# Row maxima of an attention layer folded piece by piece on GpSimd and turned on VectorE, instead of reduced on VectorE and turned on TensorE

## The chip, the cores and the metric

The kernel runs on one core of one Trainium2 chip. TensorE (PE), VectorE (DVE), ScalarE (ACT), GpSimd (POOL) and SyncE (SP, which issues nearly all DMAs here) run side by side and meet at semaphores. The metric is the device time in microseconds (us), median of several executions.

## The reference

One transformer layer in float32: attention, a layer norm, a linear layer with quantised operands, a second layer norm. Only the attention scores bear on the change:

```
# B=2 batches, H=16 heads, DK=16, L=2048, D=256
scores = einsum('bhqd,bhkd->bhqk', Q, K) / sqrt(DK)
scores = scores * tau[..., None] + delta[:, :, None, :]
attn   = softmax(scores, axis=-1)
out    = einsum('bhqk,bhkd->bhqd', attn, V)
x = layernorm(x + out @ out_w.T + out_b)
x = layernorm(x + ffn(x))
```

The softmax subtracts each query row's maximum over 2048 keys before the exponential. The kernel computes the scores twice: once with queries on the partitions, only to find the row maxima, and once with keys on the partitions, with the negated maximum already added by the matmul, for the exponential.

## The kernel before

A first block (about 250 us) makes Q, K, V, tau and delta and stores Q and K, split in high and low parts, in DRAM. The second block is the attention, with the rest of the layer at its end. Heads go in groups of 4 (`HG`), the 2048 queries of a group in 4 quarters of 512, so there are `NIT` = 32 iterations i. `q_set` and `k_set` hold two groups at a time (two heads on partitions 0 to 63, two on 64 to 127). Rows 0 to 47 of each half are the operand, two more rows of `k_set` carry delta, and rows `ROW_MAX`, `ROW_MAX`+1 of `q_set` carry the negated row maximum, high and low part.

The work of an iteration is written as 32 slots (`SLOTS`, two to each key tile k). TensorE does in a slot, in this order:

- a PV half (line 937): 8 matmuls of exponentials and values, into bank 0;
- an ST pair (line 924): two score tiles, keys on partitions, two key tiles (`AHEAD`) before they are used. So the first ST of iteration i+1 stands in slot 28 of iteration i. It waits for `rows_set`, the DMAs that bring the maxima into `q_set`. ScalarE takes each tile through the exponential (line 1069); three banks are shared, so an ST waits for the exponential three tiles back;
- what is due of a list `items` (lines 179 to 189), a hand-written order for TensorE and VectorE alike.

`items` holds for each quarter j 32 units. A unit is two score tiles with queries on the partitions (`s_unit`, line 227) into one of two bank pairs, and one VectorE reduction of both to a maximum each (`max_unit`, line 237, into `mx`). A unit may go to TensorE once VectorE has freed the pair of two items back (`s_free`). Four units (4 key chunks of 512) make the maxima of 128 queries of two heads. Units run ahead: when iteration i starts, units up to (i+1, `LEAD`) are issued, with `LEAD` 12.

Once unit (j, 31) is reduced, the maxima go to `q_set` in five steps: VectorE reduces `mx` over the 4 chunks to `nm` (`row_maxima`, line 260); GpSimd splits it in high and low (`split_max`, lines 85 and 89) into `nm_pad`; TensorE transposes `nm_pad` into a bank pair as a 33rd item "rows", after unit (j+1, 2) (`rows_turn`, line 244); VectorE copies 32 rows of it to `nm_rows` (`rows_copy`, line 252); SP issues four DMAs (`rows_store`, line 278). The last "rows" item, of j = 31, has no units beside it and is preceded by 8 score matmuls that nobody reads (`unread`, line 883).

The slot of an item follows from `due`: items in this iteration, spread evenly over the slots. With 33 items for 32 slots, slot 31 gets two. ScalarE's evacuation of bank 0 at the end of an iteration (`evacuate`, line 1058) stands in its order behind the exponentials of slot 30's ST; the first PV half of the next iteration waits for it (`att_evac`).

Other users of the queues: SP loads the next head group at the start of every fourth iteration (`group_load`, 14 DMAs, lines 165 and 168) and stores the evacuated tile (lines 1377, 1379); GpSimd copies the values of the next group in every fourth iteration (`refill`, line 1326) and normalises late chunks (line 1350). VectorE has pieces of the linear layer mixed in from iteration 27 on.

## Time and profile before

| | |
|---|---|
| runs, us | 1684.31, 1676.60, 1676.23; median 1676.6 |
| the profiled execution, us | 1681.14 |
| its span, first to last instruction, us | 1679.1 |
| mean granted TensorE clock | 0.982 |
| busy, us (share of the span) | PE 1634.2 (97%), DVE 1526.7 (91%), ACT 1311.7 (78%), POOL 127.8 (8%) |
| chain that ended last, by engine | PE 60%, DVE 23% |

Busy time of TensorE is the time in which any matmul record is open, and ends of matmuls are modelled, so a share of 97% does not say how fast it works. What follows goes by the starts of the matmuls. "Idle before" is the idle time of an engine just ahead of an instruction, with what ended it behind the arrow.

### The profile page before, as it was taken

How to read it: one execution, taken by the hardware profiler on the slowest of the kernel's cores; microseconds unless marked ns; L12 is line 12 of the kernel's file. 1: busy time of each engine (PE TensorE's matmuls, PEld its weight loads, DVE VectorE, ACT ScalarE, POOL GpSimd, SP SyncE). 2: the span in 40 equal slices, each digit the busy share in tenths (PEclk: the TensorE clock that was granted, in tenths of full speed). 3: DMA queues.
4: the chain of work that ended last, by engine and by line, in shares of the span. 5: the costliest groups of instructions: out<-in, count | busy, mean ns of one | idle time of the engine just before them, and what ended most of it. 6: DMA issues, size and time to landing. Idle time of an engine off the chain costs nothing.

```text
span 1679.1 us, 33556 instructions
## 1 busy us (share of the span) xinstructions
PE 1634.2 (97%) x13879; PEld 733.6 (44%) x13884; DVE 1526.7 (91%) x1648; ACT 1311.7 (78%) x2375; POOL 127.8 (8%) x166
## 2 busy tenths in 40 slices
PE   8999989999999999999999999999999999999987
PEld 7777753333333333333333333333333343333466
DVE  5789876999999999999999999999999989898887
ACT  3876736888888888888888888888888876678645
POOL 4222213000000000000000000000010000000110
PEclk9999996999999999999999999999999999999989
DMA  3365426000600060024003300422051001010312
GB/s 112 106 179 156 141 81 108 8 8 8 85 9 8 18 75 8 15 27 66 9 8 43 53 8 8 57 39 60 31 70 23 8 8 46 8 39 13 120 59 88
DMA packets 46960, 84.72 MB, mean 50 GB/s; under 512 B 9116, under 2 KB 21020, under 8 KB 44092
## 3 DMA queue, kind: packets, MB, share of 16 engines
q1 hardware_dynamic: 44952, 82.49, 22.9%
q8 instruction: 109, 1.79, 0.5%
q14 instruction: 43, 0.35, 0.1%
q10 hardware_dynamic: 1856, 0.09, 0.1%
HBM read 51.36 MB, written 30.67 MB: 49 GB/s over the span
## 4 chain that ended last, share of the span: by engine, by line
PE 60%; DVE 23%; issue 1%; ACT 0%; ACTq 0%; POOL 0%; DVEq 0%
PE ps L937 25%; DVE mx L237 20%; PE ps L924 20%; PE ps L227 11%; PE ps L870 2%; PE ps L868 1%; PE ps L990 1%; PE ps L244 0%; PE ps L984 0%; PE ps L867 0%; DVE stats L1173 0%; DVE work L1221 0%; DVE work L1232 0%; DVE small L1216 0%; ACT e L1038 0%
## 5 line engine op out<-in xcount | busy, mean ns | idle before, releaser
L237 DVE TENSOR_REDUCE mx<-ps 128x2 f32<-128x1024 f32 x1024 | 1226.3, 1222 | 74.8 <-PE ps L227 66.6
L1069 ACT ACTIVATE e<-ps 128x512 f32<-128x512 f32 x2048 | 1109.7, 596 | 235.4 <-PE ps L924 197.6
L937 PE MATMUL ps<-e,v_grp 128*32 128x256 f32 x8192 | 662.6, 394 | 0.3 <-issue 0.2
L924 PE MATMUL ps<-q,k 52*128 52x512 f32 x2048 | 527.2, 502 | 4.5 <-PEq L355 4.3
L227 PE MATMUL ps<-k,q 50*128 50x512 f32 x2048 | 420.2, 405 | 11.3 <-DVE mx L237 8.6
L924 PEld LDWEIGHTS ps<-q,k 52*128 52x128 f32 x2048 | 200.4, 184 | 434.1 <-ACT e L1069 390.3
L937 PEld LDWEIGHTS ps<-e,v_grp 128*32 128x32 f32 x8192 | 162.7, 108 | 358.9 <-issue 210.9
L227 PEld LDWEIGHTS ps<-k,q 50*128 50x128 f32 x2048 | 197.5, 188 | 42.6 <-DVE mx L237 32.7
L684 PE MATMUL ps<-x_p,m_p 128*128 128x512 f32 x576 | 143.9, 404 | 0.0
L684 PEld LDWEIGHTS ps<-x_p,m_p 128*128 128x128 f32 x576 | 108.2, 192 | 33.3 <-issue 9.0
L525 DVE SCALAR_TENSOR_TENSOR hid<-x_c,dw_w,hid 128x512 f32<-128x512 f32 x128 | 103.8, 861 | 15.6 <-ACT hid L466 15.5
L472 ACT ACTIVATE hid<-hid 128x512 f32<-128x512 f32 x64 | 40.5, 632 | 51.4 <-DVE hid L525 50.1
L85 POOL CAST nm_pad<-nm 128x16 fp32r<-128x16 f32 x32 | 6.7, 210 | 885.2 <-DVE nm L260 885.2
L466 ACT ACTIVATE hid<-x_c,dw_b,dw_w 128x512 f32<-128x512 f32 x64 | 46.6, 804 | 0.2
L1326 POOL COPY v_grp<-v_all 128x272 f32<-128x272 f32 x32 | 13.7, 433 | 316.8 <-PE ps L937 316.7
L870 PE MATMUL ps<-wo_t,v_all 128*128 128x256 f32 x128 | 34.0, 389 | 0.0
L707 PE MATMUL ps<-hid,pw_w 128*16 128x512 f32 x128 | 29.7, 594 | 0.0
L1350 POOL TENSOR_TENSOR v_all<-v_all 128x1024 f32<-128x1024 f32 x8 | 19.7, 2465 | 119.6 <-DMA v_all<-rz_rows 119.6
L870 PEld LDWEIGHTS ps<-wo_t,v_all 128*128 128x128 f32 x128 | 25.2, 197 | 3.7
L698 PEld LDWEIGHTS ps<-wv_p,x_p 128*128 128x128 f32 x192 | 26.1, 197 | 1.4
L698 PE MATMUL ps<-wv_p,x_p 128*128 128x256 f32 x192 | 26.7, 290 | 0.0
L990 PE MATMUL ps<-fw_p,xq_t 128*128 128x256 f32 x128 | 19.6, 310 | 7.0 <-ACT xq_t L1051 7.0
(142 smaller groups left out, 610.3 us busy)
## 6 DMA issues: line engine op xcount, KB each, us to landing
k<-k_parts SPq DMA_DIRECT2D x42, 256.0 KB
q<-q_parts SPq DMA_DIRECT2D x42, 256.0 KB
k_parts<-k_sp SPq DMA_DIRECT2D x16, 512.0 KB, 5.0
q_parts<-q_sp SPq DMA_DIRECT2D x16, 512.0 KB, 4.1
att<-ev SPq DMA_DIRECT2D x32, 256.0 KB
x_c<-in_x_t SPq DMA_DIRECT2D x8, 514.0 KB, 5.7
tau_r<-tau_rows SPq DMA_DIRECT2D x16, 256.0 KB
x_in<-in_x SPq DMA_DIRECT2D x8, 512.0 KB, 3.9
```

The lines of the kernel that those rows point to most:

```text
L227: last = nc.tensor.matmul(ps[:, s_bank(s) + half, :], q_set[r, g % 2, jh, lo + qt * P:lo + (qt + 1) * P], k_set[r, g % 2, jh, kc * CH:(kc ...
L237: nc.vector.tensor_reduce(mx[:, j % 2, :, jh, qt, kc], ps[:, b0:b0 + 2, :], AX.X, ALU.max).then_inc(s_free, 1)
L466: nc.scalar.activation(hid[:, k, c, r], x_c[:, n % 2, c, 1:1 + CH], ACT.Identity, bias=dw_b[:, k, c, r:r + 1], scale=dw_w[:, k, c, r, 1:2] ...
L472: nc.scalar.activation(hid[:, k, c, r], hid[:, k, c, r], ACT.Gelu).then_inc(gelu_done, 1)
L525: nc.vector.scalar_tensor_tensor(y_, x_c[:, n % 2, c, which:which + CH], dw_w[:, k, c, r, which:which + 1], y_, ALU.mult, ALU.add).then_in ...
L684: mm = nc.tensor.matmul(ps[:, o, :], m_p[:, kw, side, c, tap, P * o:P * (o + 1)], x_p[:, n % 2, kx_, c, tap:tap + CH], start=(m == 0), sto ...
L698: last = nc.tensor.matmul(ps[:, v_bank(n, v), D * a:D * (a + 1)], x_p[:, n % 2, kx_, c, lo:lo + P], wv_p[:, kw, c, :], start=(m == 0), sto ...
L870: last = nc.tensor.matmul(dst, a_t[p][:, c, P * a:P * (a + 1)], wo_t[:, c, :], start=False, stop=(c == CT - 1))
L924: nc.tensor.matmul(ps[:, st_bank(n), :], k_set[r, g % 2, jh, kt * P:(kt + 1) * P], q_set[r, g % 2, jh, lo:lo + CH], start=True, stop=True) ...
L937: last = nc.tensor.matmul(ps[32 * h:32 * (h + 1), 0, PVW * part:PVW * (part + 1)], v_grp[:, kt, h, :], e[:, x % E_BUFS, h * CH + PVW * par ...
L990: last = nc.tensor.matmul(tok(f_bank(n), a), xq_t[:, n % 2, a, c, :], fw_p[:, part, c, :], start=False, stop=(c == CT - 1 and part == 1), ...
L1069: nc.scalar.activation(e[:, x % E_BUFS, h * CH:(h + 1) * CH], ps[:, st_bank(n), :], ACT.Exp).then_inc(e_ready, 1)
```

## The change

- `row_maxima`, `rows_copy`, the "rows" items and `unread` are gone. An iteration has 32 items instead of 33, all units (some late iterations have others besides).
- `fold` on GpSimd: for each of the 8 groups of four units two instructions take the larger of three chunks' maxima (one column on 128 partitions each), and after a wait two more take in the fourth and negate. That is 32 instructions per quarter j, 1024 in all. Groups 3 to 7 of j = i+1 and 0 to 2 of j = i+2 are folded in iteration i, two per quarter iteration, ahead of that quarter's refill. `split_max` follows group 7.
- `rows_turn` is now a VectorE transpose of 32x32 blocks of a 128x32 tile, `nm_pad` to `nm_rows`, behind unit (j+1, 1). At the end it stands behind `gathered(0, 1)` and `gathered(0, 2)` and ahead of `z_reciprocal(dve, 1)`.
- `rows_store` is eight DMAs of 16 runs of 128 B, where it was four of 8 runs of 512 B. `q_set` is laid out by quarter and then head, so that its runs merge; a group load then has 20 DMAs instead of 14 (q by head, in runs of 2 KB where they were 8 KB).
- `LEAD` 14 (was 12), `DEFER` 2 (was 3); the units of iteration 30 are spread over 5/8 of its slots (was 3/4).

```diff
-GROUP_DMAS = 2 * (2 * TERMS + 1)
+GROUP_DMAS = 2 * (TERMS + HH * TERMS + 1)
...
-        q_set = sb(top, "q_set", [P, 2, HH, L], F32R)
+        q_set = sb(top, "q_set", [P, 2, NQ, HH, CH], F32R)
...
+                    for jh in range(HH):
+                        eng.dma_start(q_set[rows, g % 2, chunks, jh, :].bitcast(F32),
+                                      q_parts[Q_PARTS[r], b, heads.start + jh, :, cols].rearrange("d (c l) -> d c l", l=CH)).then_inc(done, 16)
...
-        LEAD = 12
-        DEFER = 3
+        LEAD = 14
+        DEFER = 2
...
-                if u == DEFER - 1 and j > 0:
-                    items.append((j - 1, "rows"))
...
+        FOLD_AHEAD = LEAD // 4
+        FOLD_ORDER = [(qt, jh) for qt in range(TT) for jh in range(HH)]
...
-        ROWS_INC = 16 * HG
+        ROWS_INC = 16 * 2 * (P // BLOCK)
...
+        def fold(pool, j, n):
+
+            qt, jh = FOLD_ORDER[n]
+            done = 2 * (len(FOLD_ORDER) * j + n + 1)
+            pool.wait_ge(s_free, unit_at[j, qt, jh, NQ - 1] + 1)
+            rows = [((half * HH + jh) * TT + qt, mx[:, j % 2, half, jh, qt]) for half in range(2)]
+            for r, parts in rows:
+                nc.gpsimd.tensor_scalar(mn[:, r:r + 1], parts[:, 0:1], parts[:, 1:2], parts[:, 2:3], ALU.max, ALU.max).then_inc(mx_folded, 1)
+            pool.wait_ge(mx_folded, done)
+            for r, parts in rows:
+                nc.gpsimd.tensor_scalar(nm[:, r:r + 1], mn[:, r:r + 1], parts[:, 3:4], -1.0, ALU.max, ALU.mult).then_inc(nm_max, 1)
...
+        def rows_turn(dve, j):
+
+            dve.wait_ge(nm_ready, j + 1)
+            if j > 0:
+                dve.wait_ge(rows_set, j * ROWS_INC)
+            nc.vector.transpose(nm_rows[:].bitcast(F32), nm_pad[:].bitcast(F32)).then_inc(nm_turned, 1)
...
+            for half in range(2):
+                row = HALF * half + ROW_MAX
+                rows = q_set[row:row + 2, g % 2, j % NQ].rearrange("t j (q l) -> t (j q) l", q=TT)
+                for b in range(P // BLOCK):
+                    first = BLOCK * b + BLOCK // 2 * half
+                    sp.dma_start(rows[:, :, BLOCK * b:BLOCK * (b + 1)].bitcast(F32), nm_rows[first:first + BLOCK // 2, :].bitcast(F32)).then_inc(rows_set, 16)
...
-                        goal = items.index((i + 2, LEAD)) if i + 2 < NIT else len(items) - 1
+                        goal = items.index((i + 2, LEAD)) if i + 2 < NIT else len(items)
                         due = goal - issued
-                        slots = SLOTS * 3 // 4 if i == NIT - 2 else SLOTS
+                        slots = SLOTS * 5 // 8 if i == NIT - 2 else SLOTS
...
-                            if u == UNITS - 1:
-                                row_maxima(dve, s)
+                            if u == DEFER - 1:
+                                rows_turn(dve, j - 1)
...
+                            for group in (FOLD_AHEAD + 2 * c, FOLD_AHEAD + 2 * c + 1):
+                                j = i + 1 + group // len(FOLD_ORDER)
+                                if j < NIT:
+                                    fold(pool, j, group % len(FOLD_ORDER))
+                                if group == len(FOLD_ORDER) - 1 and j < NIT:
+                                    split_max(pool, j)
```

**TensorE, slot 31 of iteration 1.** Before; L937 is the PV half (4 heads), L924 the ST pair, L227 the score tiles of a unit, two to each. The rows are slots 30, 31 and the PV half of the next iteration:

```order
270 L937 MATMUL ps<-e,v_grp 32x256 x4
271 L924 MATMUL ps<-q,k 128x512 x2
272 L227 MATMUL ps<-k,q 128x512 x2
273 L937 MATMUL ps<-e,v_grp 32x256 x4
274 L924 MATMUL ps<-q,k 128x512 x2
275 L227 MATMUL ps<-k,q 128x512 x4
276 L937 MATMUL ps<-e,v_grp 32x256 x4
```

Now the same slots, where L918 is the PV half and L905 the ST pair:

```order
268 L918 MATMUL ps<-e,v_grp 32x256 x4
269 L905 MATMUL ps<-q,k 128x512 x2
270 L227 MATMUL ps<-k,q 128x512 x2
271 L918 MATMUL ps<-e,v_grp 32x256 x4
272 L905 MATMUL ps<-q,k 128x512 x2
273 L227 MATMUL ps<-k,q 128x512 x2
274 L918 MATMUL ps<-e,v_grp 32x256 x4
```

The second unit of slot 31 (x4 is two units) is gone; every slot of the iteration has one.

**VectorE, the first iterations of the attention.** Before; L237 is a unit's reduction:

```order
138 L1099 UNCONDITIONAL_BRANCH
139 L237 TENSOR_REDUCE mx<-ps 128x2 x23
140 L260 TENSOR_REDUCE nm<-mx 128x16
141 L237 TENSOR_REDUCE mx<-ps 128x2 x3
142 L252 CAST nm_rows<-ps 32x128
143 L237 TENSOR_REDUCE mx<-ps 128x2 x29
```

Now:

```order
136 L1078 UNCONDITIONAL_BRANCH
137 L237 TENSOR_REDUCE mx<-ps 128x2 x24
138 L268 STREAM_TRANSPOSE nm_rows<-nm_pad 128x32
139 L237 TENSOR_REDUCE mx<-ps 128x2 x32
140 L268 STREAM_TRANSPOSE nm_rows<-nm_pad 128x32
```

Two small instructions per quarter have become one, two units behind the quarter's last reduction instead of three.

**GpSimd, a later part of iteration 3.** Before, rows of iterations 1 to 3 stand together, since GpSimd has only the two splits and the refills (L1326):

```order
63 L85 CAST nm_pad<-nm 128x4x4
64 L89 TENSOR_TENSOR nm_pad<-nm,nm_pad 128x4x4
65 L1326 COPY v_grp<-v_all 128x16x17 x2
66 L85 CAST nm_pad<-nm 128x4x4
67 L89 TENSOR_TENSOR nm_pad<-nm,nm_pad 128x4x4
68 L1326 COPY v_grp<-v_all 128x16x17 x2
```

Now, from the second refill (L1303) of iteration 3 to behind its third; L248 and L251 are the two halves of a fold:

```order
143 L1303 COPY v_grp<-v_all 128x16x17
144 L248 TENSOR_SCALAR mn<-mx 128x1 x2
145 L251 TENSOR_SCALAR nm<-mn,mx 128x1 x2
146 L85 CAST nm_pad<-nm 128x2x8
147 L89 TENSOR_TENSOR nm_pad<-nm,nm_pad 128x2x8
148 L248 TENSOR_SCALAR mn<-mx 128x1 x2
149 L251 TENSOR_SCALAR nm<-mn,mx 128x1 x2
150 L1303 COPY v_grp<-v_all 128x16x17
151 L248 TENSOR_SCALAR mn<-mx 128x1 x2
```

The split now stands behind the last fold of its quarter (rows 144, 145) and ahead of the first of the next.

## Rows read from the trace of the kernel before

**Rows 1.** The page, busy us (share of the span) xinstructions.

```profile
PE 1634.2 (97%) x13879; PEld 733.6 (44%) x13884; DVE 1526.7 (91%) x1648; ACT 1311.7 (78%) x2375; POOL 127.8 (8%) x166
```

**Rows 2.** TensorE timeline, slots 23 to 0: start us, us, engine line op out<-in xcount.

```profile
701.53 0.33 PE L244 MATMUL ps<-ident_f,nm_pad 128*128 128x128 f32 x1
701.78 0.64 PE L937 MATMUL ps<-e,v_grp 128*32 128x256 f32 x8
...
707.31 0.50 PE L924 MATMUL ps<-q,k 52*128 52x512 f32 x2
...
710.46 0.64 PE L937 MATMUL ps<-e,v_grp 128*32 128x256 f32 x8
...
711.36 0.98 PE L227 MATMUL ps<-k,q 50*128 50x512 f32 x4
712.27 0.64 PE L937 MATMUL ps<-e,v_grp 128*32 128x256 f32 x8
```

**Rows 3.** Timeline of ScalarE there.

```profile
710.38 1.08 ACT L1069 ACTIVATE e<-ps 128x512 f32<-128x512 f32 x2 [0.21 <-PE ps L924]
711.35 0.60 ACT L1058 ACTIVATE ev<-ps 128x512 f32<-128x512 f32 x1
711.83 1.10 ACT L1069 ACTIVATE e<-ps 128x512 f32<-128x512 f32 x2
```

**Rows 4.** VectorE timeline, an iteration and a half; in brackets idle before, its releaser.

```profile
661.62 0.28 DVE L252 CAST nm_rows<-ps 32x128 fp32r<-32x128 f32 x1
...
698.17 0.22 DVE L260 TENSOR_REDUCE nm<-mx 128x16 f32<-128x64 f32 x1
...
701.89 0.28 DVE L252 CAST nm_rows<-ps 32x128 fp32r<-32x128 f32 x1
703.13 21.63 DVE L237 TENSOR_REDUCE mx<-ps 128x2 f32<-128x1024 f32 x18 [0.96 <-PE ps L227]
```

**Rows 5.** Line 252 between 298 and 1352 us: duration ns min/median/max, first and last start.

```profile
L252 DVE CAST nm_rows<-ps x27: 269/278/279, 298.3 to 1351.5; 32x128 fp32r<-32x128 f32 x27
```

**Rows 6.** The same view of line 237, 400 to 1300 us.

```profile
L237 DVE TENSOR_REDUCE mx<-ps x710: 1165/1226/1229, 399.9 to 1299.5; 128x2 f32<-128x1024 f32 x178
```

**Rows 7.** Timeline of GpSimd, a split.

```profile
738.97 0.20 POOL L85 CAST nm_pad<-nm 128x16 fp32r<-128x16 f32 x1 [6.69 <-DVE nm L260]
739.25 0.22 POOL L89 TENSOR_TENSOR nm_pad<-nm,nm_pad 128x16 fp32r<-128x16 f32 x1
```

**Rows 8.** Timeline of SP's DMA issues: a group load, stores of the maxima.

```profile
585.07 1.26 SPq L165 DMA_DIRECT2D k<-k_parts  x3
...
621.66 2.58 SPq L278 DMA_DIRECT2D q<-nm_rows  x4
...
702.20 2.56 SPq L278 DMA_DIRECT2D q<-nm_rows  x4
```

**Rows 9.** Issues of two lines: duration ns min/median/max, first and last start.

```profile
L278 SPq DMA_DIRECT2D q<-nm_rows x128: 596/612/716, 236.7 to 1549.9; - x128
L387 SPq DMA_DIRECT2D tau_r<-tau_rows x16: 577/592/726, 53.6 to 227.4; - x16
```

**Rows 10.** Stretches: length, busy us by engine, PEclk, DMA share, GB/s.

```profile
84.00:86.00 2.00, 2.00 (x17) 1.87 (x16) 2.00 (x2) 0.63 (x1) 1.92 (x2) 1.00 0.74 143
...
600.00:605.00 5.00, 5.00 (x56) 1.83 (x48) 4.95 (x5) 4.39 (x9) 0.00 (x0) 1.00 0.99 116
...
610.00:615.00 5.00, 5.00 (x45) 1.80 (x42) 4.45 (x4) 3.88 (x9) 0.00 (x0) 1.00 0.55 102
```

**Rows 11.** The same view of a stretch with a store of the maxima.

```profile
661.90:665.00 3.10, 3.10 (x36) 1.21 (x28) 2.13 (x2) 2.70 (x6) 0.00 (x0) 1.00 0.03 9
```

**Rows 12.** Timeline of TensorE in iterations 30 and 31.

```profile
1545.89 1.09 PE L883 MATMUL ps<-k,q 50*128 50x512 f32 x8
...
1547.51 0.64 PE L937 MATMUL ps<-e,v_grp 128*32 128x256 f32 x8
...
1567.29 0.27 PE L867 MATMUL ps<-bias,ones 128*128 128x256 bf16 x1 [1.47 <-issue]
```

118 lines of the change are left out of this document (37 added, 81 removed).

## Prediction, made before the changed kernel ran

> **What bounds the kernel now.** First the page's busy shares [rows 1]: TensorE 97%, VectorE 91%, ScalarE 78%. Two engines are candidates, so the timelines decide. On TensorE a slot (PV half, ST pair, one unit) takes 1.24 us: from slot 24 at 701.78 to slot 31 at 710.46 there are seven, 8.68 us [rows 2], and none has a gap. VectorE, when it has something to catch up, does a reduction every 1.20 us (18 in 21.63) [rows 4]. So in a plain slot TensorE sets the pace, and VectorE has 0.04 us to spare. The granted clock is 1.00 (2.4 GHz) in all stretches shown after 600 us [rows 10, 11].
>
> An iteration without a disturbance lasts 40.27 us, from one `rows_copy` to the next (661.62 to 701.89) [rows 4]. 32 slots of 1.24 are 39.68. Of the 0.59 left, slot 31 takes 0.57: it has two units and lasts 1.81 (710.46 to 712.27) [rows 2]. The transpose stands in the place of a unit and costs about what a unit costs. The mean of 26 iterations is (1351.5 - 298.3) / 26 = 40.51 [rows 5], so 0.24 more goes to scattered waits that the change does not name.
>
> **What the change takes away.** VectorE loses 0.22 + 0.28 us of small work per iteration and the 0.96 us in which it waited because the transpose slot brought it no unit [rows 4]; it gets one transpose of 128x32, which the trace does not show. Its nearest rows are the 0.22 reduction and the 0.28 copy; I take 0.2, with 0.15 and 0.3 as ends. But VectorE does not set the pace: 32 x 1.20 + 0.2 = 38.6 against TensorE's 39.68. This saving is hidden, and the 0.3 us are worth nothing where TensorE is first.
>
> TensorE loses the 33rd item, so slot 31 has one unit. That alone would give 0.57 + 0.02 us. What is late next? **ScalarE's evacuation of bank 0.** It stands behind the exponentials of slot 30, starts at 711.35 and ends at 711.95 [rows 3]. The first PV half of the next iteration waits for it. With one unit in slot 31 that PV half would be ready at 710.46 + 1.24 = 711.70. It finds bank 0 still unread, and starts at 711.95 plus a hand-over; GpSimd's from its own instruction to the next is 739.25 - 739.17 = 0.08 [rows 7], I take 0.07. So 0.32 us of the 0.59 come back as a wait, and 0.27 stay. Today the second unit covers the evacuation entirely. ScalarE's place is fixed by slot 30's ST, which keeps its distance, so the wait does not shrink by itself.
>
> This holds for iterations 1 to 23 and 25, 24 of them: 24 x 0.27 = **6.5 us**. Iteration 24 has the item "ft" besides and keeps a double slot; in 26 the same number of other items falls due.
>
> **The rest of the sum.** Iterations 27 to 29 have VectorE full of the linear layer's work. There its small work counts: 0.5 - 0.2 = 0.3 at least, 1.3 if the 0.96 us wait goes too; I take 0.5, nearer the lower end, since other waits stand there: **1.5 us**. In iteration 30 the 8 unread matmuls start at 1545.89 and the next PV half at 1547.51 [rows 12], held up by the reduction, the split and the transpose; without them it could follow the ST at once: **1.5 us**. The chain that ends in the wait of 1.47 us at 1567.29 [rows 12] starts with that store of the maxima. It moves forward, since the last unit is issued four slots sooner (5/8 against 3/4), and SP's four further issues (2.6 us) take back half of that; so PE does not merely meet the same data later. In iteration 0 all 36 items are units (35 before), and VectorE is behind there: 1.23 + 0.2 - 0.22 - 0.28 - 0.41 of waiting is **0.5 us lost**. Sum: 6.5 + 1.5 + 1.5 - 0.5 = 9.0 us.
>
> **What is hidden, and under what.** *The way of the maxima* must end before the first ST of the next iteration, in slot 28 at 707.31 [rows 2]. Today the copy starts at 701.89, 0.11 behind the start of slot 24, SP issues from 702.20 to 704.76, and the ST is not held up [rows 2, 4, 8]. So landing takes at most 2.55 us. Now the last unit ahead of the turn is issued in slot 19 instead of 22: the turn starts 0.11 behind slot 21. That leaves 7 x 1.24 + 0.57 - 0.11 = 9.14 us. It needs 0.2 (turn) + 0.03 + 8 x 0.64 (2.56 / 4 [rows 8]) + 2.55 = 7.90. Spare: 1.24 us. The price of an issue rests on this: 8 runs cost 0.61, and `tau_r`, with 128 partitions, 0.59 [rows 9]. The number of runs doesn't set it. So 0.64 stands, and per-run pricing (1.28) is the upper end.
>
> The engines' share during a store is 0.03 over 3.1 us [rows 11]: 0.03 x 3.1 x 16 / 32 runs = 0.047 us a run of 512 B. The Trainium skill, page "DMA: Bandwidth & Descriptors", section Specifications, says that runs under 512 B are not at line rate, as the DMA engine reads, modifies and writes. No row here shows 128 B runs. By that rule I estimate 0.09 us a run; if two engines did all 128 of them, that is 6.0 us against 5.1 of issues, and the spare falls from 1.24 to 0.3. The sum stays, the rival below gets a larger chance.
>
> *GpSimd's chain.* The last reduction of a quarter ends 2.5 us ahead of the turn (two slots). The last fold and the split need 0.07 + 2t + 0.08 + 2t + 0.08 + 0.20 + 0.08 + 0.22 = 0.73 + 4t. Every small GpSimd instruction takes 0.20 to 0.22 [rows 7]; with t = 0.2 it is 1.5 us. VectorE waits from t = 0.44 on. Behind its turn are queued the reductions that free TensorE's bank pairs, with 0.8 us to spare (needed 0.91 into a slot, done at 0.08), so TensorE feels it from t = 0.65. The other seven folds lie over four slots each and cost nothing. Contention: GpSimd's copies and splits lie beside the 710 reductions between 400 and 1300 us, and none exceeds 1229 ns against a median of 1226 [rows 6].
>
> The Trainium skill, page "GPSIMD Engine Reference", section 7, gives about 102 cycles for each small read command, which does not overlap the one before. A fold has two more operands by address; at the page's 1.2 GHz I estimate t = 0.37 and a chain of 2.2 us, still under 2.5. By either the sum is the same, by the page with 0.3 us to spare.
>
> *Group loads* are 20 issues instead of 14 on SP, 6 x 0.42 (1.26 / 3 [rows 8]) = 2.5 us; behind them is queued the store of the evacuated tile, needed 40 us later. The load starts at 585.07, keeps the engines at 0.99 and ends near 612.8 [rows 8, 10]; the maxima follow at 621.66, in future some 3.5 us sooner. 5 us are spare, 19% of the load. Runs of 2 KB moved 143 GB/s at a share of 0.74, runs of 8 KB 116 at 0.99 [rows 10], so shorter runs are no dearer. In the first block SP issues 2.5 us more in four chunks, ahead of stores that are wanted a chunk later: nothing.
>
> **Rivals.**
> 1. *The evacuation does not hold TensorE up* (it starts sooner, or a scattered wait covers it). Then 24 x 0.59 = 14.2 instead of 6.5: 16.7 us in all, 1659.9. For it: 711.95 is only 0.25 behind 711.70. Against: both starts follow from the same ST.
> 2. *The maxima arrive too late*, slower than before. It decides at 1.24 us of delay, and costs as much as it is later, 31 times; from 1.24 + 9.0 / 31 = 1.53 us on the kernel is slower, an issue of 0.83 us. At 0.9 it is 31 x (2.08 - 1.24) = 26 lost, 9 gained: 1693.7. At 1.28, every issue priced by runs, 31 x 3.9 = 120: 1788. A fold of over 0.65 us leads to the same place. For it: 128 B runs and folds stand in no row. Against: rows 7 and 9.
> 3. *A new wait of the size of the gain*: some 0.3 us per iteration, from the store landing slightly late or from a tighter ScalarE, which now has only single slots to catch up in. 1672 to 1681, taken as 1676.
>
> **How the numbers follow.** The profiled execution takes 1681.1 us, 4.5 above the median of the runs. 1681.1 - 9.0 = 1672.1 for such an execution, 1676.6 - 9.0 = **1667.6 for the median**. Chances: forecast 0.53, its own range 1663 to 1673; rival 1 0.13; rival 3 0.17; rival 2 0.17. For 8 in 10 the range takes in rival 1 down to 1658 and the larger part of rival 3 up to 1679. About 0.5% (8.4 us) is what a measurement of this kernel can tell from no change; the forecast lies just beyond it. Faster: 0.33 of the forecast and rival 1, 0.46. Within: 0.20 and 0.16, 0.36. Slower: rival 2 and a rest, 0.18.
>
> **What would show it.** Iterations of about 40.0 us undisturbed, from one turn to the next; slot 31 of 1.56 us with the next PV half behind the evacuation (1.24 would be rival 1); VectorE with more idle time and no change in its 1226 ns; a fold instruction of 0.2 to 0.4 us; eight issues in about 5.1 us. An ST in slot 28 that waits for a DMA is rival 2, a turn on VectorE that waits for GpSimd its second form. The forecast is wrong above all if an issue of 16 short runs costs over 0.8 us.

## The result and the profile after

The changed kernel takes 1655.4 us in the median of four executions (1652.9 to 1667.3), beside 1677.8 for the kernel before on the same chip: a ratio of 0.9875, 95% interval 0.9835 to 0.9914. It is faster by 22.4 us. The forecast was 9.0 us; the direction was right, the size was not, and the time lies 2.6 us below the range. Later comparisons gave 0.9900 (0.9867 to 0.9934) and 0.9890 (0.9863 to 0.9917). Over all executions whose clock is on record the medians are 1656.6 us (15) and 1674.3 us (99), 17.7 us apart.

The page of the changed kernel; it answers to [rows 1]. GpSimd has 320 us more work. VectorE has no less, and its idle time fell from 152 to 122 us, where the prediction had it grow:

```profile
PE 1603.3 (97%) x13839; PEld 716.9 (43%) x13844; DVE 1528.7 (93%) x1616; ACT 1311.1 (79%) x2375; POOL 448.0 (27%) x1189
```

TensorE's timeline from slot 30 on, then ScalarE's there (columns as in [rows 2, 3]; L918 is now the PV half, L905 the ST pair, L1048 the exponential, L1037 the evacuation):

```profile
657.14 0.64 PE L918 MATMUL ps<-e,v_grp 128*32 128x256 f32 x8
...
658.38 0.64 PE L918 MATMUL ps<-e,v_grp 128*32 128x256 f32 x8
...
659.28 0.40 PE L227 MATMUL ps<-k,q 50*128 50x512 f32 x2
659.93 0.64 PE L918 MATMUL ps<-e,v_grp 128*32 128x256 f32 x8 [0.25 <-ACT ev L1037]
```

```profile
659.27 0.61 ACT L1037 ACTIVATE ev<-ps 128x512 f32<-128x512 f32 x1
```

The double slot is gone. Slot 31 lasts 1.55 us where it took 1.81, and the next PV half waits for the evacuation, as forecast (1.56). An undisturbed iteration takes 39.99 us (39.92 in another execution) against 40.27.

The new work: durations in ns min/median/max of a fold's halves, the transpose and an issue, over the whole run. Then GpSimd's last fold and split, the turn and the eight issues:

```profile
L248 POOL TENSOR_SCALAR mn<-mx x512: 347/357/1332, 220.4 to 1516.4; 128x1 f32<-128x1 f32 x171
...
L251 POOL TENSOR_SCALAR nm<-mn,mx x512: 279/291/1297, 221.2 to 1517.1; 128x1 f32<-128x1 f32 x171
...
L268 DVE STREAM_TRANSPOSE nm_rows<-nm_pad x32: 199/200/213, 231.7 to 1518.0; 128x32 f32<-128x32 f32 x32
...
L279 SPq DMA_DIRECT2D q<-nm_rows x256: 610/611/720, 233.1 to 1522.9; - x128
```

```profile
643.70 0.70 POOL L248 TENSOR_SCALAR mn<-mx 128x1 f32<-128x1 f32 x2 [3.61 <-DVE mx L237]
644.49 0.55 POOL L251 TENSOR_SCALAR nm<-mn,mx 128x1 f32<-128x1 f32 x2
645.11 0.20 POOL L85 CAST nm_pad<-nm 128x16 fp32r<-128x16 f32 x1
645.39 0.22 POOL L89 TENSOR_TENSOR nm_pad<-nm,nm_pad 128x16 fp32r<-128x16 f32 x1
```

```profile
645.99 0.20 DVE L268 STREAM_TRANSPOSE nm_rows<-nm_pad 128x32 f32<-128x32 f32 x1
```

```profile
646.22 5.21 SPq L279 DMA_DIRECT2D q<-nm_rows  x8
```

Two numbers below need a definition. An **iteration** i runs from the start of evacuation i-1 to that of i. The **level** of a kernel is its time at a mean granted clock of 0.988: executions of one kernel differ in their clock (0.978 to 0.992 in the kernel before) and in time with it, and one least-squares line through all executions but those of fold3 and pad8, with a level of its own for each kernel, gives 1.20 us per 0.001, with a scatter of 1.8 us around it. Levels have a standard error of 0.2 for the kernel before, 0.5 for the changed one (1672.2 and 1657.6, 14.7 apart) and 0.6 to 1.1 for the others. A level takes out what a kernel gains or loses through the clock, also where its own waits move the clock. The versions ran on different chips; the kernel before, which ran beside each of them, has levels of 1671.8 to 1673.5 on the five chips.

### The profile page after: what moved, and what is told of

Read it like the earlier page. It is cut to its first block, busy times and chain, and to the rows that moved or that the text cites. A ratio compares the mean times of both kernels' runs of the same rounds, so it can differ in the third digit from the quotient of the medians.

```text
span 1651.1 us, 34599 instructions
## 1 busy us (share of the span) xinstructions
PE 1603.3 (97%) x13839; PEld 716.9 (43%) x13844; DVE 1528.7 (93%) x1616; ACT 1311.1 (79%) x2375; POOL 448.0 (27%) x1189
## 4 chain that ended last, share of the span: by engine, by line
PE 67%; DVE 14%; ACT 2%; issue 2%; ACTq 0%; DVEq 0%
PE ps L918 30%; PE ps L905 23%; PE ps L227 12%; DVE mx L237 10%; PE ps L864 1%; ACT e L1048 1%; ACT ev L1037 1%; DVE stats L1149 1%; PE ps L862 1%; DVE work L1208 0%; DVE work L1197 0%; DVE small L1192 0%; PE ps L861 0%; DVE work L1205 0%; DVE xq L1211 0%
## 5 line engine op out<-in xcount | busy, mean ns | idle before, releaser
L237 DVE TENSOR_REDUCE mx<-ps 128x2 f32<-128x1024 f32 x1024 | 1239.1, 1223 | 49.7 <-PE ps L227 36.9
L1048 ACT ACTIVATE e<-ps 128x512 f32<-128x512 f32 x2048 | 1109.0, 596 | 207.6 <-PE ps L905 167.0
L918 PE MATMUL ps<-e,v_grp 128*32 128x256 f32 x8192 | 655.8, 392 | 5.8 <-ACT ev L1037 5.8
L905 PE MATMUL ps<-q,k 52*128 52x512 f32 x2048 | 525.6, 500 | 4.5 <-PEq L355 4.3
L227 PE MATMUL ps<-k,q 50*128 50x512 f32 x2048 | 414.5, 399 | 4.5 <-DVE mx L237 3.9
L248 POOL TENSOR_SCALAR mn<-mx 128x1 f32<-128x1 f32 x512 | 180.5, 359 | 847.4 <-DVE mx L237 847.1
L905 PEld LDWEIGHTS ps<-q,k 52*128 52x128 f32 x2048 | 200.0, 184 | 430.7 <-ACT e L1048 388.0
L918 PEld LDWEIGHTS ps<-e,v_grp 128*32 128x32 f32 x8192 | 161.7, 108 | 377.7 <-issue 202.7
L227 PEld LDWEIGHTS ps<-k,q 50*128 50x128 f32 x2048 | 196.8, 187 | 18.4 <-DVE mx L237 10.3
L251 POOL TENSOR_SCALAR nm<-mn,mx 128x1 f32<-128x1 f32 x512 | 141.7, 289 | 25.2
L89 POOL TENSOR_TENSOR q_sp<-qx,q_sp 128x512 fp32r<-128x512 f32 x16 | 20.5, 1284 | 69.6 <-ACT q_sp L515 69.0
L89 POOL TENSOR_TENSOR x_p<-x_c,x_p 128x1028 fp32r<-128x1028 f32 x8 | 19.4, 2420 | 61.4 <-ACT x_p L460 61.3
```

Source lines behind the costliest of these rows:

```text
L227: last = nc.tensor.matmul(ps[:, s_bank(s) + half, :], q_set[r, g % 2, j % NQ, jh, qt * P:(qt + 1) * P], k_set[r, g % 2, jh, kc * CH:(kc + ...
L237: nc.vector.tensor_reduce(mx[:, j % 2, :, jh, qt, kc], ps[:, b0:b0 + 2, :], AX.X, ALU.max).then_inc(s_free, 1)
L248: nc.gpsimd.tensor_scalar(mn[:, r:r + 1], parts[:, 0:1], parts[:, 1:2], parts[:, 2:3], ALU.max, ALU.max).then_inc(mx_folded, 1)
L251: nc.gpsimd.tensor_scalar(nm[:, r:r + 1], mn[:, r:r + 1], parts[:, 3:4], -1.0, ALU.max, ALU.mult).then_inc(nm_max, 1)
L905: nc.tensor.matmul(ps[:, st_bank(n), :], k_set[r, g % 2, jh, kt * P:(kt + 1) * P], q_set[r, g % 2, i % NQ, jh, :], start=True, stop=True). ...
L918: last = nc.tensor.matmul(ps[32 * h:32 * (h + 1), 0, PVW * part:PVW * (part + 1)], v_grp[:, kt, h, :], e[:, x % E_BUFS, h * CH + PVW * par ...
```

## The experiments

| kernel | executions | median us | level us |
|---|---|---|---|
| before | 99 | 1674.3 | 1672.2 |
| layout_only | 10 | 1677.8 | 1671.8 |
| no_unread | 10 | 1672.6 | 1672.0 |
| before_slots58 | 10 | 1673.8 | 1670.2 |
| item_back | 10 | 1670.3 | 1668.7 |
| filler | 7 | 1665.5 | 1662.3 |
| evac_early | 10 | 1665.2 | 1661.8 |
| slots_back | 10 | 1664.2 | 1660.1 |
| dve_extra | 4 | 1665.1 | 1658.6 |
| warm | 6 | 1658.9 | 1658.5 |
| after | 15 | 1656.6 | 1657.6 |
| st_first | 4 | 1657.8 | 1657.2 |
| combo30 | 6 | 1658.0 | 1656.6 |
| warm30 | 6 | 1654.1 | 1656.0 |
| lead_back | 3 | 1709.2 | 1693.3 |
| fold3 | 1 | 1782.3 | - |
| pad8 | 1 | 1850.9 | - |

### Both kernels once more: how much is chance

> The kernel before, unchanged, once more. In the two profiled executions TensorE's granted clock stayed at 1.2 GHz at the start of the attention until 281 us in the kernel before and until 261 us in the changed one, although both had stood idle 4.3 us just ahead of the first ST: some 8 us of the 28 us between the two spans. Theory A (chance): the length of that stretch varies between executions of the same kernel; this run then shows it ending anywhere between 260 and 281 us, and the evacuation of iteration 0 starts near 299 us in some. Theory B (the change does it): it ends at about 281 us again and that evacuation starts at 307 us, within 1 us. Undisturbed iterations stay at 40.27 us under both.

> The changed kernel, unchanged, once more. Theory A: the low-clock stretch at the start of the attention ends anywhere between 260 and 281 us, and a time near 1667 us among the runs (one of four had it, at a clock of 0.980 instead of 0.991) is an execution in which it was long. Theory B: it ends at 261 us, the evacuation of iteration 0 starts at 298 us, and the times are near 1655 us. Undisturbed iterations 39.99 us under both, with VectorE's reductions at a median of 1226 ns.

Theory A holds. (A third batch of the changed kernel, expected at 1655 to 1659 us and 14 to 17 below the kernel before, took 1656.9, 18.0 below it.) Stretches of 4 us (columns as in [rows 10]: length, busy us of the five engines, PEclk, DMA share, GB/s) of the first profile of before, of this one, and of the changed kernel:

```profile
256.00:260.00 4.00, 4.00 (x24) 1.21 (x18) 1.23 (x1) 1.79 (x5) 0.00 (x0) 0.50 0.63 200
...
276.00:280.00 4.00, 4.00 (x25) 1.20 (x17) 2.24 (x2) 1.59 (x4) 0.00 (x0) 0.50 1.02 123
280.00:284.00 4.00, 4.00 (x38) 1.40 (x36) 3.53 (x3) 3.34 (x7) 0.00 (x0) 0.91 0.82 115
```

```profile
256.00:260.00 4.00, 4.00 (x28) 1.31 (x24) 1.23 (x1) 1.79 (x4) 0.00 (x0) 0.50 0.95 239
260.00:264.00 4.00, 4.00 (x40) 1.38 (x44) 3.66 (x3) 2.98 (x7) 2.11 (x5) 0.93 1.08 166
```

```profile
256.00:260.00 4.00, 4.00 (x26) 1.40 (x24) 2.45 (x2) 1.90 (x4) 0.31 (x1) 0.50 1.00 150
260.00:264.00 4.00, 4.00 (x38) 1.25 (x36) 3.04 (x3) 2.95 (x6) 3.56 (x8) 0.83 1.09 122
```

At the start of the attention TensorE runs at 1.2 GHz for some slots of 2.16 us instead of 1.24. Their number is 11 in the first profile of before, 2 in this one, and 3, 2 and 11 in three profiles of the changed kernel; over all kernels it went from 2 to 14. From the first ST to the first evacuation it took 55.51 and 47.61 us before, 48.66, 47.64 and 55.46 after; less 0.92 per slow slot that is 45.4, 45.8, 45.9, 45.8 and 45.3. So 8 x 0.92 = 7 us of the difference between the first profile of before and the first of the changed kernel come from such a stretch that happened to be long, and iteration 0 itself has not changed.

### The layout of the queries alone

```diff
-        q_set = sb(top, "q_set", [P, 2, HH, L], F32R)
+        q_set = sb(top, "q_set", [P, 2, NQ, HH, CH], F32R)
...
+                    for jh in range(HH):
+                        eng.dma_start(q_set[rows, g % 2, chunks, jh, :].bitcast(F32),
```

> The kernel before, with only the new layout of the query operand (quarter, then head) and the group load in 20 DMAs with runs of 2 KB; the maxima go their old way. The iterations with a group load (4, 8, 12, 16, 20, 24) gained 0.65 to 1.1 us each between the kernels, 0.27 in the plain ones between them. Theory A (shorter runs collide less with what TensorE and VectorE wait for): those iterations gain 0.4 to 0.8 us here too, 2.5 to 5 us in all, and the time is 1672 to 1674. Theory B (the gain there came from the slack that the single slots give): nothing, 1677 to 1678, and the load's issues take 11 to 12 us where they took 6. The prediction had the load as free.

The ratio is 1.0013 (0.9984 to 1.0043), the level 0.4 us lower: nothing, as forecast. Iteration 4, with a load, takes 40.35 us where two profiles of before have 40.72 and 40.27, iteration 16 40.75 against 40.92 and 40.26: no more than executions differ.

### The 33rd item, and what of it costs

item_back, in the changed kernel:

```diff
+                if u == DEFER - 1 and j > 0:
+                    items.append((j - 1, "gap"))
...
+            nc.tensor.transpose(ps[:, s_bank(s), 0:P], ident_f[:], ident_f[:]).then_inc(s_full, 1)
...
+            nc.vector.tensor_copy(spare[:], ps[0:2 * HG * TT, s_bank(s), 0:P]).then_inc(s_free, 1)
```

> The changed kernel with a 33rd item per iteration again: TensorE transposes the identity matrix into a bank pair behind unit 1 and VectorE copies 64 rows of it to a buffer that nobody reads. The maxima keep the new way. The forecast's step (the double slot 31 covers the evacuation, single slots cost its wait): undisturbed iterations return from 39.99 to 40.27 us, no wait for the evacuation in the PV half behind slot 31, 24 x 0.28 = 6.7 us slower, 1662. Rival (the item also caused the scattered waits, through VectorE's wait for the item without a unit, and the gains in iterations 27 to 31): about 10 to 14 us slower than the changed kernel, 1665 to 1669, and the iterations with a group load lose over 0.28 us each. If the 8 us of iteration 0 belong to neither, they stay as they are.

Its level is 11.2 us above the changed kernel's. TensorE's slot 31, then VectorE:

```profile
423.02 0.64 PE L941 MATMUL ps<-e,v_grp 128*32 128x256 f32 x8
423.59 0.51 PE L928 MATMUL ps<-q,k 52*128 52x512 f32 x2
423.93 0.99 PE L230 MATMUL ps<-k,q 50*128 50x512 f32 x4
424.86 0.64 PE L941 MATMUL ps<-e,v_grp 128*32 128x256 f32 x8
```

```profile
410.83 0.28 DVE L282 COPY spare<-ps 32x128 f32<-32x128 f32 x1
411.99 6.18 DVE L240 TENSOR_REDUCE mx<-ps 128x2 f32<-128x1024 f32 x5 [0.87 <-PE ps L230]
```

Undisturbed iterations return to 40.27, there is no wait for the evacuation, and VectorE's wait of 0.9 us for the next unit is back. In its profile iterations 1 to 23 take 929.6 us against 922.8: these 6.8 us are the main term. In all the rival's size holds, 10 to 14 us: the item costs more than the 6.7 us of its undisturbed iterations.

The double slot has a wait of its own. TensorE loads weights ahead of each matmul (PEld); here are the loads for the second unit of slot 31 in the kernel before, whose bank pair VectorE frees at 711.80, with the end of a reduction:

```profile
711.84 0.19 PEld L227 LDWEIGHTS ps<-k,q 50*128 50x128 f32 x2 [0.52 <-DVE mx L237]
```

The second unit starts 0.48 us behind the first, where a unit leaves TensorE for the next work after 0.33 (711.36 and, in slot 24, 702.69 to 703.02). So about 0.15 of slot 31's 0.57 us is a wait for VectorE and not TensorE's work.

dve_extra puts two small VectorE instructions behind each turn, filler two matmuls into TensorE's slot 31; neither goes through a bank pair:

```diff
+                                nc.vector.tensor_reduce(spare_r[:], ident_f[:, 0:64].rearrange("p (a b) -> p a b", b=4), AX.X, ALU.max)
+                                nc.vector.tensor_copy(spare[:], ident_f[:])
```

```diff
+                                if k == KT - 1 and jh == 1 and i < NIT - 1:
+                                    filler(HG * (x + 1 + AHEAD), (i + 1) // NQ)
```

> The changed kernel with two more small instructions on VectorE behind each turn, a reduction of 128x64 to 128x16 and a copy of 128x128, whose results nobody reads: about the 0.5 us that VectorE did for the maxima before, without TensorE's 33rd item. The prediction held that VectorE's small work is hidden in the plain iterations and counts only from 27 to 29. Then undisturbed iterations stay at 39.92 to 39.99 us, iterations 26 to 29 take 0.5 to 1.5 us more in sum, and the whole is 1 to 2 us slower than the changed kernel. Rival: VectorE has so little to spare that the iterations with other VectorE work or with a group load (4, 8, 17, 20, 22, 24) lose too, 0.3 to 0.5 us each, and much of the 11 us that the item put back cost was this: 4 to 6 us slower.

> The changed kernel with two score-like matmuls at the end of slot 31, into the bank of the next ST tile, that nobody reads: TensorE's work of the 33rd item is back, but nothing passes through a bank pair or VectorE. Theory (the item's price is its place in the bank pairs and VectorE's rhythm, not its matmuls): the extra 0.33 us lies under the wait for the evacuation (0.18 to 0.25 us), undisturbed iterations 39.95 to 40.1 us, 1 to 3 us slower than the changed kernel at an equal clock. Rival (any work in slot 31 costs what it takes): 40.27 us again, 7 to 11 us slower.

VectorE's small work costs 1.0 us (error 1.0) and leaves undisturbed iterations at 39.99: hidden, as forecast. filler costs 4.8 us (error 0.8), 3.8 of it in iterations 1 to 23 of its profile; undisturbed ones take 40.09 to 40.16. Its two matmuls are not the item's work exactly: they stretch slot 31 to 1.71 us, where the item has 1.81. So work of TensorE alone and work of VectorE alone come to some 6 of the item's 11.2 us. What is left points to the item's place in the bank pairs, in which TensorE and VectorE wait for each other, as the row above shows it in slot 31; no run isolates that place.

### Can the wait for the evacuation be had back?

evac_early moves the evacuation ahead of the second exponential of slot 30, st_first one ST tile ahead of the PV half that waits:

```diff
-                            if i > 0 and kt == AHEAD - 1 and jh == 0:
-                                evacuate(i - 1)
+                                if i > 0 and kt == AHEAD - 1 and jh == 0 and half == 0:
+                                    evacuate(i - 1)
```

```diff
+                                early_st = i > 0 and k == 0 and jh == 0
+                                if early_st:
+                                    st(x + AHEAD, jh, (0,))
                                 pv_half(i, k, jh)
```

> The changed kernel with ScalarE's evacuation of bank 0 between the two exponentials of slot 30's ST pair instead of behind both. If the prediction's step is right that single slots leave TensorE waiting for this evacuation (0.25 us before the PV half behind slot 31, undisturbed iterations 39.92 to 39.99 us), the evacuation starts 0.49 us sooner, that wait goes and an iteration takes 39.7 us: 24 x 0.25 = 6 us faster than the changed kernel. Rival: the second exponential, now 0.6 us later, holds up the ST pair of slot 31 or of slot 0, which takes its bank: the wait only moves, 0.0 to 0.35 us per iteration, and the time is the same or up to 3 us slower.

> The changed kernel with the first of the two ST tiles of slot 0 ahead of the first PV half instead of behind it, in iterations 1 to 31. The PV half waits for ScalarE's evacuation either way (it starts 1.55 us behind the PV half of slot 31, where a slot is 1.24), but TensorE fills 0.17 us of that wait with a tile that is due anyway and whose bank is free since slot 30's exponentials. Theory (the wait for the evacuation is the end that counts, as the prediction has it): undisturbed iterations 39.75 to 39.82 us instead of 39.92 to 39.99, 24 x 0.17 = 4 us faster than the changed kernel. Rival: as with the evacuation moved ahead, the exponentials of slot 31 (behind the evacuation) hold the second tile, so the 0.17 us comes back there: no change.

evac_early is 4.2 us slower (error 0.8), with undisturbed iterations of 40.12 us: its rival's mechanism, at somewhat more than the rival's 3 us. ScalarE, then TensorE:

```profile
711.70 0.60 ACT L1037 ACTIVATE ev<-ps 128x512 f32<-128x512 f32 x1 [0.19 <-PE ps L918]
```

```profile
711.00 0.64 PE L918 MATMUL ps<-e,v_grp 128*32 128x256 f32 x8
...
712.35 0.64 PE L918 MATMUL ps<-e,v_grp 128*32 128x256 f32 x8
712.92 0.90 PE L905 MATMUL ps<-q,k 52*128 52x512 f32 x2
```

The evacuation now waits for slot 31's own PV half, which ends at 711.64. Slot 31 takes 1.35 instead of 1.55 us. With the evacuation behind this PV half it can't be shorter than their sum: 0.64 for the PV half, 0.60 for the evacuation, two hand-overs. The ST pair behind it takes 0.90 instead of 0.50, as it waits for the exponential that was put back, and slot 0 lasts 1.64 instead of 1.24. st_first shows iterations of 39.77 and of 39.99 us and no difference in time (level 0.4 lower, error 1.0). An evacuation in two halves, the first behind slot 30's PV half, was not tried: TensorE would write a bank while ScalarE reads it.

### How much room the maxima have

```diff
-        LEAD = 14
-        DEFER = 2
+        LEAD = 12
+        DEFER = 3
```

> The changed kernel with LEAD 12 and DEFER 3 again: the last unit ahead of the turn is issued in slot 21 instead of 19, the turn stands behind unit 2, so 0.11 behind slot 24. That leaves 707.31 - 701.89 = 5.42 us of slots until the first ST of the next iteration, and the turn (0.2), eight issues of 0.65 (5.2) and a landing of at most 2.55 us need up to 7.95. By the prediction's pricing of the maxima's way the ST waits 2.0 to 2.5 us in each of 31 iterations: undisturbed iterations of 41.5 to 42.3 us, 1720 to 1735 us in all, slower than the kernel before. Rival: the landing is much shorter than its bound of 2.55 us (1 us or less): the ST waits 0.9 us or less, iterations of 40.3 to 40.9 us, 1665 to 1685 us. Third: nothing happens, because the wait is hidden by the two key tiles of lead: 1657.

The rival holds for the wait (0.96 us, iterations of 40.96), but its time of 1665 to 1685 us does not: the median of three executions is 1709.2. A fourth, at a clock of 0.962, took 1730.2 us and is left out of the table (with it the level is 1694.7). Turn, issues and ST:

```profile
707.17 0.20 DVE L268 STREAM_TRANSPOSE nm_rows<-nm_pad 128x32 f32<-128x32 f32 x1
```

```profile
707.40 5.21 SPq L279 DMA_DIRECT2D q<-nm_rows  x8
```

```profile
713.70 0.50 PE L905 MATMUL ps<-q,k 52*128 52x512 f32 x2 [0.96 <-DMA q<-nm_rows]
```

From the turn to the ST it is 6.53 us: 0.23, the issues 5.21, and a landing of 1.09 behind the last issue, not 2.55. In the changed kernel the turn at 645.99 stands 9.23 us ahead of the ST at 655.22, so 2.7 us are spare. pad8 uses them up with eight more DMAs of the same form ahead of the eight:

```diff
+            for n in range(8):
+                sp.dma_start(pad_rows[2 * n:2 * n + 2], nm_rows[0:BLOCK // 2, :].bitcast(F32)).then_inc(pad_done, 16)
```

> The changed kernel with eight more DMAs of 16 runs of 128 B in each store of the maxima, ahead of the eight, to a buffer that nobody reads. With the wait of 0.96 us at a lead of three slots less, the way of the maxima is 6.5 us from the turn to the ST (turn 0.2, issues 5.2, landing 1.1), against 9.1 us until the ST: 2.6 us to spare, not the 1.24 of the prediction. Eight more issues are 5.2 us, so the ST should wait 2.6 us in each iteration: undisturbed iterations of 42.3 to 42.6 us, 1740 to 1760 in all. By the prediction's bound of 1.24 us to spare it would be 4.0 us per iteration, 43.9, near 1790. Rival: the DMAs overlap or queue otherwise, and the landing is longer than 1.1 us with twice the descriptors: in between.

fold3 does every fold instruction three times:

```diff
+            for m in range(2):
+                for h2, (r, parts) in enumerate(rows):
+                    nc.gpsimd.tensor_scalar(mn2[:, 2 * m + h2:2 * m + h2 + 1], parts[:, 0:1], parts[:, 1:2], parts[:, 2:3], ALU.max, ALU.max)
```

> The changed kernel with every fold instruction on GpSimd done three times (twice into columns that nobody reads). A fold's two halves take 0.71 and 0.55 us now, so the last fold, the split and the hand-overs are 2.0 us against the 2.5 us that stand between the last reduction and the turn. Tripled it is 2.0 + 2 x 1.26 = 4.5 us: the turn on VectorE waits 2.0 us, the reductions queued behind it give TensorE its bank pairs, and 0.8 us of that are to spare. By the prediction's threshold TensorE loses 1.2 us per iteration or a little less: undisturbed iterations of 40.7 to 41.2 us, 1685 to 1700 in all, slower than the kernel before. Rival: VectorE makes up the delay in the slots ahead of the turn and TensorE's wait stays under 0.3 us: 1660 to 1668.

TensorE's waits in pad8 and in fold3 (us in total, times, longest):

```profile
PE ps L912 <- DMA q<-nm_rows: 77.8, 31, 4.4
```

```profile
PE ps L230 <- DVE mx L240: 74.2, 38, 17.7
```

77.8 / 31 = 2.51 us in pad8, where 5.2 - 2.7 = 2.5 was to be expected from lead_back. fold3's undisturbed iterations take 41.37 us, 1.4 more, near the 1.2 of the threshold at 0.65 us a fold (17.7 of its 74.2 us are one wait ahead of iteration 0). But the times, of one execution each, are 1850.9 and 1782.3 us, 116 and 51 above the changed kernel's 1656.6 with the waits added. Two stretches of pad8 show why:

```profile
440.00:445.00 5.00, 2.50 (x20) 0.70 (x12) 1.93 (x2) 1.84 (x4) 0.13 (x1) 0.70 0.46 74
445.00:450.00 5.00, 5.00 (x30) 1.90 (x28) 2.89 (x3) 2.60 (x5) 1.65 (x5) 0.50 1.07 114
```

TensorE stands still for half of the first and works at 1.2 GHz in the second; iterations 1 to 25 take 42.5 to 52.6 us. The mean clock is 0.908, that of fold3 0.952, that of lead_back 0.980 to 0.972, where the changed kernel has 0.988. By the line of 1.20 us per 0.001, carried on far beyond the executions it was fitted to, the clock would be worth some 96 of the 116 us and 43 of the 51: an estimate.

### The end of the attention

slots_back has 3/4 in the changed kernel, before_slots58 5/8 in the kernel before, no_unread leaves the 8 unread matmuls out of the kernel before:

```diff
-                        slots = SLOTS * 5 // 8 if i == NIT - 2 else SLOTS
+                        slots = SLOTS * 3 // 4 if i == NIT - 2 else SLOTS
```

```diff
-                            unread(s_bank(s), 4)
```

> The changed kernel with the units of iteration 30 spread over 3/4 of its slots again instead of 5/8. The prediction had the gain at the end (1.5 us in iteration 30, and half of the chain to the wait at 1567 us kept) come from the earlier last unit. If so, iteration 31 gets 1 to 2.5 us longer and the others do not move: 1 to 2.5 us slower than the changed kernel. Rival: iteration 30 is shorter (42.07 instead of 43.81 us) because the 8 unread matmuls are gone, whatever the slots, and the ST of iteration 31 has room: no change in the sum of iterations 30 and 31 beyond 0.5 us.

> The kernel before with the units of iteration 30 in 5/8 of its slots. The changed kernel with 3/4 was 2.5 us slower than with 5/8 at an equal clock, and its iteration 30 took 6 us more, since the first ST of iteration 31 waited 3.4 us for the maxima. Theory A: the earlier last unit is a gain by itself, so the kernel before gets faster too, 1 to 2.5 us. Theory B: before, four issues instead of eight leave the maxima in time at 3/4 already, and 5/8 only compensates for the longer way; then nothing changes (within 1 us), iterations 30 and 31 together stay at 92.6 to 95.5 us.

> The kernel before without the 8 score matmuls that nobody reads in iteration 30; the last transpose item and everything else stay. Item_back kept the short iteration 30 (42.08 us) without them, and both profiles of the kernel before have 43.81. Theory: these matmuls are the 1.5 us of the prediction's step for iteration 30; without them it takes 42.1 to 42.5 us and the rest is the same, 1.5 us faster than before. Rival: what holds up the next PV half is the way reduction, split, transpose through three engines, and the unread matmuls only fill the wait: 43.8 us again, and perhaps a lower clock behind the idle time.

slots_back is 2.5 us slower at an equal clock (error 0.8). The first ST of iteration 31 waits there for the maxima, and the clock falls behind it:

```profile
1531.65 0.79 PE L905 MATMUL ps<-q,k 52*128 52x512 f32 x2 [3.38 <-DMA q<-nm_rows]
```

before_slots58 is 2.0 us faster than the kernel before at an equal clock (error 0.6): the shorter spread is a gain by itself, of about 2 us in either kernel. no_unread leaves iteration 30 at 43.82 us. Its rival holds: the matmuls only fill the time in which reduction, split and transpose go through three engines, and the 1.75 us there (43.81 to 42.07) went with that way. lead_back bears this out: with the lead of 12 again its iteration 30 takes 42.08 us too. With the units in 5/8 of the slots the kernel before has 43.34, so 1.3 of the 1.75 are left to the way alone.

### The low clock at the start of the attention

Without added matmuls TensorE stands still for 4.26 to 4.28 us ahead of the first ST in every profile, at the end of the first block. warm and warm30 put 20 and 30 unread matmuls there (`range(10)` and `range(15)`); combo30 has st_first's edit besides.

```diff
+                for m in range(15):
+                    for half in range(2):
+                        r = rows_of(half, K_S)
+                        nc.tensor.matmul(ps[:, s_bank(PRE) + half, :], q_set[r, 0, 0, 0, 0:P], k_set[r, 0, 0, 0:CH], start=True, stop=True)
```

> The changed kernel with 20 score-like matmuls at the end of the first block, in the 4.3 us in which TensorE waits there for the other engines before the first ST; nobody reads them. In the profiles the granted clock is 1.2 GHz from 248 us on for 2 to 14 slots of 2.16 us instead of 1.24, and that length varies from one execution to the next in every kernel. Theory (the low clock follows the idle time): without the idle time the first slots take 1.24 us, the times lie closer together (a spread of 5 us instead of 15), and the median is 3 to 8 us lower than the changed kernel's, 1650 to 1654. Rival: the clock falls there for another reason, or the matmuls delay the end of the block: the same times, or 1 us more.

> The changed kernel with 30 unread matmuls at the end of the first block instead of 20. The 20 took 2.56 us (0.128 each, two at a time), and TensorE still waited 1.78 us ahead of the first ST; the granted clock was 1.2 GHz for 11 slots afterwards. With 30 they take 3.84 us and 0.5 us of idle time stay. Theory (the idle time brings the low clock, and 1.78 us were enough for it): slots of 1.24 us from the start, iteration 0 some 3 to 12 us shorter than in the changed kernel, 1650 to 1654 us. Rival (the clock falls whatever TensorE does there): 2 to 14 low slots again, 1657 to 1659, no gain.

> The same, with the first ST tile of slot 0 ahead of the first PV half in iterations 1 to 31. That edit alone gave plain iterations between 39.77 and 39.99 us and, at an equal clock, 0.4 us less than the changed kernel, within what could be told. Expected 0 to 3 us below the kernel with the 30 matmuls alone. The rival is no difference.

The theory falls. warm leaves 1.78 us of idle time, 11 slow slots and a level 0.9 above the changed kernel's. In combo30 only 0.68 us of idle time are left, and fourteen slow slots followed; warm30, with the same 0.69, had two:

```profile
249.49 0.70 PE L910 MATMUL ps<-q,k 52*128 52x512 f32 x3 [0.68 <-PEq L355]
```

```profile
252.00:256.00 4.00, 4.00 (x23) 1.47 (x22) 0.39 (x1) 2.86 (x7) 0.84 (x3) 0.50 0.54 177
...
280.00:284.00 4.00, 4.00 (x24) 1.20 (x16) 2.25 (x2) 1.85 (x4) 0.71 (x2) 0.50 0.29 45
```

The level of warm30 is 1.6 us below the changed kernel's (error 0.9), that of combo30 0.9: no version is shown to beat it. What sets the length of the stretch stays open.

## Why the prediction was right or wrong

The table holds mean us per stretch, from four profiles of the kernel before (layout_only and no_unread among them, which are no different at an equal clock) and three of the changed one. "Less low clock" is the difference with the low clock taken out of both, at 0.92 of 2.16 us, as in the slots of iteration 0.

| stretch | before | changed | difference | less low clock | forecast |
|---|---|---|---|---|---|
| iteration 0, less slow slots | 45.6 | 45.7 | 0 | 0 | +0.5 |
| 1 to 23 | 931.8 | 922.8 | -9.0 | -9.0 | -6.2 |
| 24 to 26 | 124.0 | 123.4 | -0.6 | -0.6 | -0.3 |
| 27 to 29 | 151.4 | 145.6 | -5.9 | -5.4 | -1.5 |
| 30 and 31 | 93.7 | 91.9 | -1.9 | -1.5 | -1.5 |
| behind the last evacuation | 69.6 | 69.6 | 0 | - | 0 |

**Right.** TensorE sets the pace. Slot 31 loses its second unit, the wait for the evacuation takes its place, and 0.28 to 0.35 us per undisturbed iteration remain, where 0.27 was forecast. item_back and evac_early confirm both halves. Rival 1 did not come true: the changed kernel's time is near rival 1's 1659.9 us, but the wait for the evacuation is there, 24 times and 5.8 us in all. VectorE's saving is worth nothing in the steady part (dve_extra), a reduction still takes 1226 ns beside 1024 folds, an issue does not go by its runs (0.611 and 0.61 us; forecast 5.1 us for eight, measured 5.2), and group loads are hidden, although their issues take 12 us instead of 6, where 2.5 us more were forecast. The Trainium skill, page "GPSIMD Engine Reference", section 7, had led to an estimate of 0.37 us for a fold instruction with two operands by address: L248, which has two, agrees with 0.357; L251 has one of them and takes 0.291. The Trainium skill, page "DMA: Bandwidth & Descriptors", section Specifications, had led to an estimate of 6.0 us for the transfer of the short runs. Here the issues were the limit: eight more such DMAs in pad8 make the ST wait 2.51 us, as their issues ask (5.2 - 2.7), where transfers of 6.0 us would ask for 3.3.

**Mis-sized: the item.** The forecast had 6.5 us for it in the undisturbed iterations, which item_back's profile bears out with 6.8 in 1 to 23. The step that failed is the next one: 0.5 us per iteration in 27 to 29, "nearer the lower end, since other waits stand there", 1.5 in all. These iterations fell by 5.4 us less low clock, and putting the item alone back costs 3.8 of them: 1.3 per iteration, the upper end, which the prediction kept for the case that VectorE's wait for the item without a unit counts too. VectorE's small work alone, the lower end (0.9 for three iterations), brings back 0.7 (dve_extra). With 1.0 in 24 to 26 the item's terms add up to 11.6 us, beside 11.2 of the levels.

**Mis-sized: the scattered waits.** "0.24 more goes to scattered waits that the change does not name" was priced at nothing, and 2 us went there. What iterations 1 to 23 take beyond undisturbed ones fell from 5.6 to 3.6 us. item_back leaves it at 3.4, and layout_only has no gain, so neither the item nor the layout did it. The lead or the new way of the maxima remain, and no run separates them.

**At an equal clock** the gain is 14.7 us: 11.2 for the item and 3.5 (error 0.6) for the rest, of which the end of the attention fills 3.3, 2.0 for the shorter spread (before_slots58) and 1.3 for the way through three engines. The table's differences less low clock add up to 16.5, from few profiles; the two counts agree to 2 us and no better.

**Iterations 27 to 29.** Before, TensorE waited there for VectorE, and its clock fell behind the wait:

```profile
1429.45 0.50 PE L227 MATMUL ps<-k,q 50*128 50x512 f32 x2 [1.68 <-DVE mx L237]
```

```profile
1428.00:1432.00 4.00, 2.55 (x22) 0.86 (x22) 3.97 (x5) 1.96 (x4) 0.10 (x1) 0.88 0.00 0
1432.00:1436.00 4.00, 4.00 (x23) 2.39 (x21) 1.51 (x3) 1.16 (x3) 0.00 (x0) 0.69 0.00 0
```

But the changed kernel has such a place too, in iteration 29:

```profile
1464.00:1468.00 4.00, 2.55 (x16) 1.10 (x15) 3.73 (x4) 1.30 (x3) 1.25 (x4) 0.78 0.02 4
1468.00:1472.00 4.00, 4.00 (x28) 2.12 (x29) 1.37 (x3) 1.60 (x4) 0.00 (x0) 0.79 0.00 0
```

The low clock lasts 3.4, 6.8, 3.4 and 13.7 us there in the four profiles of before and 3.4, 6.8 and 6.8 in the three of the changed kernel, so it makes only 0.5 us of the difference. Less low clock the profiles lie close together: 147.4 to 149.7 us before (mean 148.5), 142.9 to 143.4 for the changed kernel (mean 143.1). item_back's one profile has no low clock there and 146.9 us. TensorE's waits for a reduction at line 227 fell in these iterations from 12 (7.2 us) to 4 (3.2 us) between the first profiles, its waits of any kind from 7.2 to 5.5. Of the 5.4 us the item so has 3.8. For the 1.6 left the lead of 14 units or the way of the maxima remains; lead_back has 148.4, with 3.1 us of waits for the DMA in it, which points to the lead. This last step is argued, not shown.

**Iterations 30 and 31** came out by the forecast's size, and by its two causes: the three-engine way (no_unread) and the earlier last unit (slots_back, before_slots58). Iteration 0 lost nothing, where 0.5 us was forecast.

**The comparison itself.** At an equal clock the gain is 14.7 us, of which the forecast has 9.0. The other 7.7 of the measured 22.4 us are put down to the clocks of the executions compared; of the four of before only one clock is on record (0.982). Over all executions 3.0 stay (17.7), 1.9 of it because the changed kernel's mean clock is higher, 0.9877 against 0.9861, at 1.20 us per 0.001; the rest was chance, to which the forecast gave no width. Over all executions the changed kernel's 1656.6 us still lie 1.4 below the range. Of that, 2.3 us are the base: the forecast took off from 1676.6 us, the median of three executions, where 99 have 1674.3. The gain of 14.7 us for 9.0 is not chance: its terms are those above.

**Rival 2** was priced too low, not too high. It decides at 2.7 us of delay and not at 1.24, since the landing was taken at its bound, but once it sets in it costs more than its waits, through the clock: lead_back waits 32 us and is 36 slower at an equal clock, and 53 in the median.

## What to carry to other kernels

A small item that passes through a shared bank pair can cost more than its instructions (here 11.2 us, where work put on either engine alone cost 4.8 and 1.0): count its place in the rotation too, above all where the reader is behind. When the item that filled a slot goes, look for the next wait in that slot: here it gave back half of the slot and left the rest. Before a difference of 1% is explained, compare several executions at an equal granted clock, and price a wait on TensorE at the granted clock of the slots behind it too.

## What the runs showed that was not expected

- At the start of the attention TensorE works at 1.2 GHz for 2 to 14 slots, 2 to 13 us of time, differently in each execution, and filling the idle time ahead down to 0.7 us does not settle it.
- A wait of 2.5 us in each iteration went with a mean clock of 0.908 and cost 116 us beyond the waits, in one execution.
- A GpSimd instruction on 128x1 with two operands by address takes 357 ns, with one 291, where a copy of 128x16 takes 200.
- Unread score matmuls on the two row halves ran at 0.128 us each (2.56 us for 20), while filler's two on one half held TensorE up for 0.47 us (slot 31 of 1.71 us instead of 1.24).
